# One maxima product of 320 columns per head, one PSUM bank for outputs and sums in turn, centred weights and a new time table

## The reference, cut to what matters

```python
def layer(x):                                  # x: 2 x 8192 x 512
    x = x + layernorm(attention(layernorm(x)))
    return x + layernorm(ffn(layernorm(x)))    # layernorm: (x - mean) / sqrt(var + 1e-5)

def attention(x):                              # 16 heads of 32, windows of 64 tokens
    q, k, v = split(x @ w_qkv)
    # local: each query sees the 64 keys from 32 before it to 31 after it
    local = softmax(where(near, q @ k_near.T * scale, -1e9)) @ v_near
    # global: each query sees every 64th key of its sequence, 128 of them
    glob = softmax(q @ k[:, ::64].T * scale) @ v[:, ::64]
    return (local + glob) @ w_out + b_out

def ffn(x):                                    # one fixed linear map of 512 features
    return real(ifft(fft(x) @ (w_real + 1j * w_imag))) + bias
```

## Time and profile before

| | us |
|---|---|
| median of 3 runs | 3582.44 |
| lowest, highest | 3581.54, 3588.01 |
| span of the profiled execution | 3584.1 |
| PE busy | 3478.6 (97%) |
| DVE, POOL, ACT busy | 2311.2, 2222.2, 1977.0 |
| DMA, mean share of 16 engines, 1400 to 3400 us | 0.66 |

### The profile page before, as it was taken

One profiled execution on the slowest core, in us unless ns is written; L12 is line 12 of the kernel. 1 busy time (PEld: TensorE's weight loads), 2 busy tenths in 40 slices (PEclk: granted clock), 3 DMA queues, 4 the chain that ended last, 5 costly groups with the idle time before them and its releaser, 6 DMA issues.

```text
span 3584.1 us, 79850 instructions
## 1 busy us (share of the span) xinstructions
PE 3478.6 (97%) x29010; PEld 2683.5 (75%) x29010; DVE 2311.2 (64%) x4796; ACT 1977.0 (55%) x4132; POOL 2222.2 (62%) x3475
## 2 busy tenths in 40 slices
PE   8999999999997999999999999999999999999997
PEld 6888888888886677777777777777777777777774
DVE  5444444444434577777777777777777777777774
ACT  3222222222223567776676767777677767777674
POOL 1000000000001688889888898888988888988887
PEclk9999999999997899999999999999999999999999
DMA  6877887787777566666666666666666666666641
GB/s 176 240 224 210 228 235 221 209 236 229 216 236 172 131 147 155 147 150 155 150 152 147 153 152 151 150 148 155 154 150 146 151 153 157 149 144 151 153 117 42
DMA packets 493810, 603.94 MB, mean 169 GB/s; under 512 B 51080, under 2 KB 260120, under 8 KB 493480
## 3 DMA queue, kind: packets, MB, share of 16 engines
q1 hardware_dynamic: 413512, 564.80, 61.9%
q10 hardware_dynamic: 79680, 34.70, 5.4%
q0 software_dynamic: 288, 0.08, 0.0%
HBM read 361.59 MB, written 203.23 MB: 158 GB/s over the span
## 4 chain that ended last, share of the span: by engine, by line
PE 41%; POOL 17%; ACT 4%; issue 3%; ACTq 2%; DVE 1%; DMA 1%; POOLq 0%; SPq 0%; DVEq 0%
PE ps_misc L1118 11%; PE ps_sc L1049 5%; PE ps_ml L1025 4%; PE ps_mg L1030 4%; PE ps_o L1077 3%; PE ps_sc L1063 3%; PE ps_s L1096 3%; PE ps_o L1102 3%; POOL qk L809 3%; PE ps_s L1090 2%; POOL qk L812 2%; POOL qk L806 2%; ACTq L892 2%; POOL xb L842 2%; POOL ot_lo L827 2%
## 5 line engine op out<-in xcount | busy, mean ns | idle before, releaser
L937 DVE TENSOR_REDUCE mx<-ps_ml 128x2 f32<-128x384 f32 x1024 | 559.5, 546 | 334.5 <-PE ps_ml L1025 327.3
L499 PE MATMUL po<-ht_hi,w_both 128*128 128x512 f32 x2048 | 639.3, 391 | 1.6 <-ACT ht_hi L290 1.5
L897 ACT ACTIVATE ps_ml<-mask 128x384 f32<-128x384 bf16 x1022 | 500.1, 491 | 235.0 <-issue 116.2
L869 ACT ACTIVATE qk<-ps_sc 128x384 f32<-128x384 f32 (+1 forms) x1024 | 415.6, 458 | 210.6 <-PE ps_sc L1049 209.5
L499 PEld LDWEIGHTS po<-ht_hi,w_both 128*128 128x128 f32 x2048 | 385.2, 188 | 88.6 <-issue 6.5
L940 DVE TENSOR_REDUCE mx<-ps_mg 128x2 f32<-128x256 f32 x1024 | 424.7, 415 | 2.1 <-PE ps_mg L1030 1.9
L499 PE MATMUL po<-ht_lo,w_both 128*128 128x512 f32 x1024 | 399.0, 390 | 0.0
L882 ACT ACTIVATE v<-ps_sc 128x512 f32<-128x512 f32 x512 | 302.6, 592 | 93.7 <-PE ps_sc L1063 82.6
L806 POOL TENSOR_SCALAR_AFFINE_SELECT qk<-qk 128x512 f32<-128x512 f32 (+1 forms) x512 | 298.2, 582 | 87.6 <-ACT qk L869 85.0
L809 POOL TENSOR_SCALAR_AFFINE_SELECT qk<-qk 128x512 f32<-128x512 f32 x512 | 324.9, 635 | 35.0
L858 ACT ACTIVATE xb<-xb,nmb,rsb 128x512 f32<-128x512 f32 x384 | 310.4, 809 | 53.8 <-POOL nmb L799 53.5
(11 more groups left out here) (149 smaller groups left out, 8738.6 us busy)
## 6 DMA issues: line engine op xcount, KB each, us to landing
xb<-in_L_attn_x SPq DMA_DIRECT2D x256, 256.0 KB, 5.7
w_both<-q_hi_d SPq DMA_DIRECT2D x256, 256.0 KB
ks<-k_hi_d SPq DMA_DIRECT2D x128, 288.0 KB
q_lo_d<-o_lo SPq DMA_DIRECT2D x32, 1024.0 KB, 8.6
k_lo_d<-o_lo SPq DMA_DIRECT2D x32, 1024.0 KB, 10.1
w_both<-q_lo_d SPq DMA_DIRECT2D x128, 256.0 KB
vw<-v_d SPq DMA_DIRECT2D x128, 256.0 KB, 2.9
out<-xb SPq DMA_DIRECT2D x128, 256.0 KB, 3.3
```

What stands on the lines that cost most here:

```text
L499: last = nc.tensor.matmul(po[bank(o, u)][:], wa[:, k, o * P:(o + 1) * P], ha[u][:, k, :], start=start, stop=stop)
L869: nc.scalar.activation(p_loc[:, i, 2 * hp:2 * hp + 2, lo:MW], ps_sc[n % 2][:, 0:2 * MW].rearrange("p (h n) -> p h n", h=2)[:, :, lo:MW], A ...
L897: nc.scalar.activation(ps_ml[u % 2][:, :, 0:MW], mask[:].rearrange("p (o n) -> p o n", o=1).to_broadcast([P, 2, MW]), ACT.Copy).then_inc(s ...
L937: nc.vector.tensor_reduce(mx[s % 2][:, 0, heads, tile], ps_ml[u % 2][:, :, 0:MW], axis=AX.X, op=ALU.max).then_inc(ml_taken, 1)
```

## The change

**Maxima.** In the key stack each head's columns now hold keys 0 to 127, the 128 global keys, keys 128 to 383, the global keys again, keys 384 to 575 (832 columns). Any tile's 192 local keys and the global ones then lie in 320 columns side by side. One product of 320 columns per head (L1111) takes the place of the 192 and the 128. Two heads of a unit write two banks, `ps_mx` is four banks in all. The seed writes 2 x 320 (mask and zeros), and one reduce gives five maxima of 64 columns per head (L1007). Three small DVE operations per step join them (`maxc`).

**Outputs and sums.** `ps_o` and `ps_s` become one bank `ps_os`, used in turn: local outputs (`ol`, one block), copied out by ACT, local sums (`sl`) and global sums (`sg`), turned by DVE, global outputs (`pvgo`), scaled. The local sums take four windows of columns (192, 192, 128, 64) where they took six; the columns are as many. The buffer of local exponentials is free again after `sl` only.

**Norms.** The rows of `w_out`, of m, and the two biases have their means taken off once. The layer norms behind `out` and `ffn` then need no mean: one DVE operation each (`x1`, `za`) multiplies by 1/sqrt and adds x. The ACT norms `y` and `z`, the POOL adds `ya` and `za` and two of three L799 go.

**Loads.** Keys of a step come in three runs, so 9 DMAs for 3; global keys and values are loaded once per sequence, the bias row in 3 of 16 chunks only. Values have three buffers for four. x of the next chunk is asked for right behind the store of a tile.

**Table.** All times are new, with a period of 16.5 for a step, and exponentials, masks, adds and reduces have times of their own.

```diff
-        ps_ml = [pb(f"ps_ml{b}", [P, 2, 256]) for b in range(2)]
-        ps_mg = pb("ps_mg", [P, 4, P])
+        ps_mx = [pb(f"ps_mx{b}", [P, 2, 512]) for b in range(2)]
...
-        ps_o = pb("ps_o", [P, 512])
-        ps_s = pb("ps_s", [P, 512])
+        ps_os = pb("ps_os", [P, 512])
...
-        MAXIMA = (-12.7446, -11.7884, -10.8921, -9.3495, -8.4672, -7.7699, -6.8344, -5.6171)
...
+        PERIOD = 16.5
+            "max": (-24.872, -26.24, -16.256, -15.775, -14.46, -21.059, -13.3, -12.287),
...
+                    if name == "x_loc":
+                        n, tile, hp = unit(s, "loc", i), i // 2, i % 2
+                        lo = WIN if tile == 0 else 0
+                        act.wait_ge(sc_scored, n + 1)
+                        at_least(act, sl_done, s)
...
+                        turn = (i // 2 + 1) % 2
+                        nc.scalar.activation(ps_mx[u % 2][:, :, 0:MWG], mask[:, turn:turn + 1, :].to_broadcast([P, 2, MWG]),
+                                             ACT.Copy).then_inc(seeded, 1)
...
+                        nc.vector.tensor_reduce(mb[s % 2][:, heads, tile, :],
+                                                ps_mx[u % 2][:, :, 0:MWG].rearrange("p h (b n) -> p h b n", n=WIN), axis=AX.X,
+                                                op=ALU.max).then_inc(mx_taken, 1)
...
+                    if name == "x1":
+                        dve.wait_ge(rs_done[0], n)
+                        dve.wait_ge(x_loaded[i], (s + 1) * 16)
+                        nc.vector.scalar_tensor_tensor(xb[:, i, :], yb[:, i, :], rs[0][:, i:i + 1], xb[:, i, :],
+                                                       ALU.mult, ALU.add).then_inc(x1_done, 1)
...
+                        at_least(pe, seeded, u - 1)
+                        for n in range(2):
+                            last = nc.tensor.matmul(ps_mx[u % 2][:, n, 0:MWG],
+                                                    qs[g][0:ROWS_MAX, 2 * pair + n, tile * P:(tile + 1) * P],
+                                                    ks[g][0:ROWS_MAX, 2 * pair + n, WINDOW_AT[tile]:WINDOW_AT[tile] + MWG],
+                                                    start=False, stop=True, skip_group_check=True)
+                        last.then_inc(mx_scored, 1)
...
+                    if name == "sl":
+                        pe.wait_ge(o_copied, s + 1)
+                        pe.wait_ge(s_added, 3 * s + 3)
+                        pe.wait_ge(loc_masked, 4 * s + 4)
+                        pe.wait_ge(last_masked, s + 1)
```

More of the change, by code:

```diff
@@ L18 @@
 from concourse import mybir
+from collections import defaultdict
 from contextlib import ExitStack
@@ L333, in _ @@
                 chunks(act, body, first)
-                act.wait_ge(spec_loaded[1], 16)
-                for k in range(KT):
-                    nc.scalar.activation(wo_hi[:, k, :], wo[:, k, :], ACT.Copy).then_inc(split_hi, 1)
                 act.wait_ge(row_made, 1)
@@ new lines, in attention_phase @@
+        STEP = {
+            "max": (-24.872, -26.24, -16.256, -15.775, -14.46, -21.059, -13.3, -12.287),
+            "maxr": (-19.664, -21.916, -23.238, -16.846, -14.4, -16.935, -12.923, -12.007),
+            "seed": (-27.437, -25.389, -19.575, -21.413, -18.549, -15.991, -11.851, -5.285),
+            "maxc": (-8.043,),
+            "mt": (-7.075,),
+            "x_mt": (-7.321,),
+            "loc": (1.227, 2.047, 2.487, 4.879, 4.523, 2.713, 6.54, 9.124),
+            "x_loc": (6.805, -1.467, -3.201, 1.238, 4.857, 11.708, 1.494, 3.961),
+            "locm": (3.04, 1.84, 10.046, 9.347),
+            "sadd": (3.089, 10.537, 11.992),
+            "last": (2.119,),
+            "x_last": (8.31,),
+            "lastm": (6.018,),
+            "glob": (4.978, 14.416, 4.971, 17.04),
+            "x_glob": (14.986, 6.641, 3.522, -2.455),
+            "ol": (15.617, 15.303),
+            "oc": (13.129,),
+            "sl": (18.147,),
+            "sg": (18.716,),
+            "sums": (19.823,),
+            "pvgo": (21.449,),
+            "rglob": (21.034,),
+            "ogm": (27.239,),
+            "rloc": (22.758,),
+            "olm": (22.76,),
+            "osum": (29.096,),
+        }
@@ L734, in attention_phase @@
+            return [it[1:] for it in items]
+        SCORED = {"mt": "x_mt", "loc": "x_loc", "last": "x_last", "glob": "x_glob", "tr": "x_tr"}
         ORDER = timeline()
-        UNITS = [(*it, hp) for it in ORDER if it[0] in ("loc", "glob", "last", "mt", "tr") for hp in range(1 + (it[0] == "loc"))]
+        UNITS = [it for it in ORDER if it[0] in SCORED]
         UNIT_AT = {u: n for n, u in enumerate(UNITS)}
-        unit = lambda s, name, i, hp=0: UNIT_AT[name, s, i, hp]
-        LAST_USE = max((("loc", 3, 1), ("last", 0, 0), ("glob", 3, 0)), key=lambda use: unit(GROUPS, *use))
+        unit = lambda s, name, i: UNIT_AT[name, s, i]
@@ L739, in attention_phase @@
+        exps = iter((SCORED[name], s, i) for name, s, i in UNITS)
+        ORDER = [next(exps) if it[0] in SCORED.values() else it for it in ORDER]
+        LAST_USE = max((("loc", 7), ("last", 0), ("glob", 3)), key=lambda use: unit(GROUPS, *use))
         MISC = [it for it in ORDER if it[0] in ("out", "ffn") and it[2] % KT == 0]
@@ new lines, in item @@
+                    if name == "x_loc":
[3 more added lines that the diff above has]
+                        at_least(act, sl_done, s)
+                        nc.scalar.activation(p_loc[:, tile, 2 * hp:2 * hp + 2, lo:MW],
+                                             ps_sc[n % 2][:, 0:2 * MW].rearrange("p (h n) -> p h n", h=2)[:, :, lo:MW],
+                                             ACT.Exp, scale=SCALE).then_inc(sc_exped, 1)
@@ L1087, in item @@
-                        for n, (sums, windows) in enumerate(parts):
+                        for tile in O_PARTS[i]:
+                            if tile < 4:
+                                pe.wait_ge(loc_masked, 4 * s + tile + 1)
+                            else:
+                                pe.wait_ge(last_masked, s + 1)
+                            for h in range(4):
+                                rows, head = slice(h * DH, (h + 1) * DH), slice(h * DH, (h + 1) * DH)
+                                if tile < 4:
+                                    x0, w = (0, P) if tile == 0 else (P * tile - WIN, MW)
+                                    last = nc.tensor.matmul(ps_os[rows, x0:x0 + w], vw[s % V_BUFS][:, tile, head], p_loc[:, tile, h, MW - w:MW],
+                                                            start=tile == 0, stop=False, skip_group_check=True)
+                                else:
+                                    last = nc.tensor.matmul(ps_os[rows, CHUNK - WIN:CHUNK], vl[s % V_BUFS][:, head], p_last[:, h, :],
+                                                            start=False, stop=True, skip_group_check=True)
```

496 lines of the change are left out of this document (263 added, 233 removed).

## The result

| | time, us (median, lowest to highest) | to the kernel before | span of the profiled run |
|---|---|---|---|
| before | 3582.53 (3581.54 to 3588.01) | 1 | 3584.1 |
| after | 3491.02 (3485.56 to 3494.99) | 0.9738, 95% interval 0.9723 to 0.9753 | 3493.2 |
| predicted | 3382 (3318 to 3477) | 0.944 | |

The change is faster by 91 us, where 200 were predicted. The sign is right, and the time lies 14 us above the range.

A forecast was written before the change was run, and what follows sets the result against it. PE was taken as the bound: 18.57 - 0.95 (maxima) - 0.1 (outputs and sums) - 0.5 (waits) = 17.0 us a step. Over 127 steps that saves 199 us, the ends 1: 3382 us, range 3318 to 3477.

The forecast's parts named there:

- the part on the other engines: Work per step beside PE's 17.0 us: DVE 14.8, ACT 13.2, POOL 14.0 or less, DMA no more than 12.3.
- Three small joins at under 0.2 each, +0.6: On DVE, the three small operations joining the maxima add 0.6 us a step, each under 0.2.
- So all four fit under PE, and each edit of theirs costs nothing by itself: DVE, ACT, POOL and DMA all stay below PE's 17.0 us a step, so their edits add no time.
- Maxima: On PE, two 320-column products a unit cost 0.31 to 0.36 us, saving 0.95 us a step; the largest term.
- Outputs and sums: On PE, the new blocks of output and sum products take 2.6 us a step for 2.71: -0.1.
- Waits: PE's weight loads wait 1.45 us a step for exponentials; half returns, less 0.25 of new waits: -0.5, bounds -1.3 and +0.4.
- The fused norms: On DVE, two fused adds priced at 692 ns add 1.4 us a step; POOL falls to 14.0 or less.
- Ends: Outside the repeated steps: centring and first loads +3 us, last tile -3, or -4 with a freer POOL; -1 in the total.
- A helper sets the pace: Rival: two banks of maxima circling PE, DVE, ACT lose 0.1 us a unit, 17.8 a step, 3483; with dear shape 0.19.
- One bank: Rival: serial uses of `ps_os` with slow hand-overs make it slower, 19.1 us a step, 3650; chance 0.05.
- All waits covered: Rival: PE needs 16.2 us a step, but the local exponentials' circle holds it at 16.2 to 16.5, 3318 us; chance 0.13.

The follow-up runs named there:

- the mended kernel: The changed kernel with the third small DVE join of the maxima made a one-input reduction instead of a two-input maximum: 3392.45 us, ratio 0.9466.

## Why the prediction was wrong

**The step that failed** is in the part on the other engines: "Three small joins at under 0.2 each, +0.6", and the sentence that closes it, "So all four fit under PE, and each edit of theirs costs nothing by itself". I priced an instruction of 16 elements by its size. Two of the three took 0.17 us; the third took 1.37. With it and the fused adds DVE came to 16.0 us a step for 14.8, and the stall fell at a fixed place ahead of operations that PE waits for. Put right alone, the time is 3392, 10 us from the forecast, so 99 of the 109 us between forecast and result are this one term. No trace row of before could give it: its second phase has no DVE instruction with two SBUF inputs. It should have been bounded from above, by the GpSimd operations it could meet, 0.64 to 1.28 us each; as measured, up to two of them one behind the other.

That the mended kernel is within 10 us of the forecast is in part luck: the terms below err in both directions. The prediction expected to fail in the waits of PE, and not here.

**Maxima: right.** Units of two products of 320 columns cost 0.31 to 0.36 by the forecast. The timeline of PE in after:

```profile
2051.72 1.40 PE L1167 MATMUL ps_os<-qk,vw 128*32 128x128 f32 x32
2053.05 0.32 PE L1170 MATMUL ps_os<-p_last,vl 64*32 64x64 f32 x8
2053.30 0.50 PE L1215 MATMUL ps_misc<-ht_hi,w_both 128*128 128x512 f32 x1
...
2054.64 0.46 PE L1111 MATMUL ps_mx<-w_both 97*128 97x320 f32 x2
2054.94 0.34 PE L1133 MATMUL ps_sc<-w_both,ks 99*128 99x128 f32 x2
2055.34 1.08 PE L1186 MATMUL ps_os<-qk,ones 128*32 128x192 f32 x24
2056.35 0.32 PE L1186 MATMUL ps_os<-p_last,ones 64*32 64x64 f32 x8
2056.59 0.56 PE L1111 MATMUL ps_mx<-w_both 97*128 97x320 f32 x2
2056.99 0.34 PE L1133 MATMUL ps_sc<-w_both,ks 99*128 99x128 f32 x2
```

A unit takes 2054.94 - 2054.64 = 0.30 here and 0.40 behind the 32-column sums. One product to the next is 154 ns in the median, and the wide product undone in the mended kernel priced the term at 0.95 us a step, as forecast. Added up from start to start, the maxima cost 3.71 us a step from 1400 to 3400 us before and 2.66 from 1400 to 3300 in the mended kernel.

**Outputs and sums: wrong sign, small.** They cost 2053.30 - 2051.72 = 1.58 and 2056.59 - 2055.34 = 1.25, together 2.83. The forecast had 2.6, and before it was 2.71. So by these steps the term is +0.12 for -0.1. The interpolation "128 about 0.235" held where another window follows (0.24 in the outputs, median). What was left out is the window ahead of the products of `p_last`: there 128 columns cost 0.33, and three windows of 192 cost 1.09 for 1.02. The changes back to wide products cost 0.11 for 0.09. Over the long stretches, waits included, outputs and sums went from 2.89 to 2.82 us a step; 0.13 of the 2.89 is the wait for the add L812.

**Waits: right in size once the join is mended, and wrong in place.** 18.57 - 0.95 + 0.12 = 17.74, and the mended kernel needs 17.10: waits and the rest gave 0.64 for the 0.5 taken. With the slow join a step takes 17.91, so the stall ate all of it and 0.17 more. But the weight-load waits that the forecast meant to halve didn't fall. In the mended kernel they are 1.67 us a step, for 1.45 before:

```profile
PEld ps_sc L1153 <- ACT qk L933: 93.2, 112, 0.8
PEld ps_sc L1134 <- ACT p_last L940: 92.2, 110, 0.8
```

And yet they cost PE next to nothing: there a 512-column product is followed by the next wide product after 0.23 us in the median, whichever that is. Before, the wait for `glob` was free too (0.23 us from the product ahead to L1063). Only the one for `last` cost something: 0.57 us from the product ahead to L1057 for 0.23 elsewhere, 0.34 us a step. These 0.34 and the 0.13 for L812 are what the new order gave back. The forecast's reason, `last` standing too close behind two exponentials on ACT, was right. But "I take half" of the 1.45 took a base that mostly cost nothing, so that the size came out is in part luck.

**The fused norms: mis-sized.** 805 and 830 ns for the 692 taken from an addition with one PSUM operand, 0.25 us a step together. They too have two SBUF inputs. The shortest is 0.70, and where one lies beside a GpSimd mask with an add behind it (29 of 128 of L1072) the median is 1.19. Their load on POOL is gone as forecast: 14.1 us a step for 14.0.

**Ends.** -7 us for the -1 forecast. No run takes it apart.

**The rivals.** "A helper sets the pace" gave 3483, the nearest of all numbers, with the engine (DVE) right. Its mechanism, the two banks of maxima going round too slowly, isn't what happened: in the mended kernel the same banks go round with the same reduce and seed, 0.81 and 0.71, at 17.10 us a step. "One bank" didn't decide: with the joins mended, the named waits of PE's products for `ps_os` are 0.3 us in 1900. "All waits covered" isn't what the mended kernel shows either: its PE stands at 99.6% and its named waits are 3 us, but that is at 17.1 us a step and not 16.2 to 16.5, since the 1.3 us of weight-load waits that this rival took off were for the most part not costing PE anything.

**The range** was cut at 17.75 us a step inside a rival that I had given 0.19. The result, 17.91, lies in the part that was cut off.

## What to carry to other kernels

Price a small instruction by what it can be made to wait for, not by its size. If DVE reads two SBUF tiles while GpSimd is busy, write it as a reduction over one tile, or give it a PSUM operand (the bias addition L1046 of one PSUM and one SBUF tile takes 675 to 693 ns in all 128 cases of after, 31 of them beside L889 and L897), or put it where GpSimd waits. DVE takes its work in order and is 88% busy in the mended kernel: a stall of 1.1 to 1.2 us cost the step 0.8, whether or not anybody waited for the stalled result. When an edit of the bound engine gives less than its price (71 for 120 us), look for what else makes that engine wait before doubting the price.

## What the runs showed of the hardware

**A two-input DVE instruction and GpSimd keep each other out.** The maximum of two SBUF tiles of 128 x 16 takes 186 to 190 ns alone and 0.96 to 1.93 us where it meets GpSimd's 512-element operations; the same as a reduction of one tile 186 to 196 ns, at any time. A mask with one input (L883, or L889 with the join moved) holds it as an add or a product of two tiles does. The join ends 37 to 49 ns behind the end of a GpSimd operation in 125 of 128 cases. Often that isn't the one it started in: in 91 it lets a second one pass, which GpSimd starts with no gap (61 times L883 behind L897, 30 times L897 behind L889), and in 32 the first one releases it. In the 91 the join gets in where GpSimd's next operation starts 68 to 85 ns behind the end, and no join is passed over at such a gap; but in the 32 it gets in with no gap. Why it is passed over in the one case and not in the other is open. It works both ways. GpSimd's add of 256 columns (L893 in after) takes 735 ns on the average in the cases that overlap no such DVE instruction and 981 in those that do, and the mask (L886) 638 and 755. With both fused norms undone and the join a reduction, these rows are back at 734 and 637 on the average, as before the change.

The Trainium skill (SBUF — State Buffer, Who interferes with whom) has this rule: a DVE instruction with two inputs in SBUF contends with a GpSimd instruction that reads SBUF, through a port pair that one of them holds at a time, and a reduction never does on this chip. The runs agree that the form with two inputs is held up and the reduction isn't; the ports themselves stand in no trace, and every GpSimd operation named here reads SBUF. Had I weighed the rule in the prediction, it would have named L1020, L1053 and L1072. The Trainium skill (SBUF — State Buffer, Summary: rules for kernel authors) says of a DVE instruction with two SBUF inputs that the second one to issue is blocked until the first one finishes. By that the join should have run at the end of L897, at 2047.11 in the timeline above. It ended at 2047.73, 0.03 behind L883, so it can wait for two.

**The granted clock.** From 1400 to 3300 us it was 0.99 to 1.00 of 2.4 GHz in all runs but the one with both norms undone, where it was 0.95. In that run PE, busy 1720 of the 1900 us, idles more than in any other, and the clock falls to 1.2 GHz again and again, for 3 to 7 us at a time. Its mean over the whole run is 0.956, for 0.991 in the mended kernel. If PE had had work in all of that time, the difference would be some 130 of the 408 us (an estimate, 3.5% of 3790, and an upper bound); how much of it is the clock wasn't separated.
